# A six-layer decoder on one core: first statistics and normalising inside the weights' block, ones set by Pool, gates behind the split of x

## What is computed

```python
def _L0_attn_ref(hidden_states, Wq, Wk, Wv, Wo, gate):
    q, k, v = hidden_states @ Wq.T, hidden_states @ Wk.T, hidden_states @ Wv.T
    q = q * cos + rotate_half(q) * sin            # k likewise
    k_feat, q_feat = elu(k) + 1.0, elu(q) + 1.0
    memory = einsum('bhsd,bhse->bhde', k_feat, v)
    mem_out = einsum('bhsd,bhde->bhse', q_feat, memory) / denom
    attn = softmax(q k^T * scale) v
    g = sigmoid(gate)
    combined = g * mem_out + (1.0 - g) * attn
    return combined @ Wo.T

x = x + _L0_attn_ref(_layernorm(x), ...)          # layer 1: attention_linear
x = x + _L0_xattn_ref(ctx_512, _layernorm(x), ...)
x = x + _L0_ffn_ref(_layernorm(x), ...)
x = x + _L1_attn_ref(_layernorm(x), ...)          # layers 4 and 5: attention_layers
x = x + _L1_xattn_ref(_layernorm(x), ctx_512, ...)
x = x + _L1_ffn_ref(_layernorm(x), ...)
```

## Time and profile before

| | us |
|---|---|
| median of 3 runs | 3126.85 (3123.44 to 3128.61) |
| the profiled execution | 3120.07 |
| its span in the trace | 3118.0 |
| weights' block of attention_linear, by its rows | 3.4 to 25.6 |
| start of the main block to the first projection | 26.4 to 46.6 |
| weights' block of attention_layers | 1550.8 to 1615.3 |

### The profile page before, as it was taken

One profiled execution on the slowest core, in us unless ns is written; L12 is line 12 of the kernel. 1 busy time (PEld: TensorE's weight loads), 2 busy tenths in 40 slices (PEclk: granted clock), 3 DMA queues, 4 the chain that ended last, 5 costly groups with the idle time before them and its releaser, 6 DMA issues. The chain is left out here.

```text
span 3118.0 us, 34900 instructions
## 1 busy us (share of the span) xinstructions
PE 2474.1 (79%) x12662; PEld 1641.7 (53%) x12662; DVE 1844.8 (59%) x2916; ACT 1240.6 (40%) x1869; POOL 849.6 (27%) x1197
## 2 busy tenths in 40 slices
PE   5899989863532342999727999999999969999999
PEld 4454545321211122999624445545555537888887
DVE  4666665628977851777556777566555525444443
ACT  2343434328645531666411434334333313333332
POOL 1222222215567754333252343000111110000000
PEclk8899999975665565999858999999999978999999
DMA  2313132227222133899676656333433314001000
GB/s 92 85 42 82 42 82 45 68 86 283 73 68 80 52 96 121 283 305 302 213 206 158 153 155 160 92 95 91 119 97 88 99 52 178 14 28 41 1 28 14
DMA packets 200953, 340.40 MB, mean 109 GB/s; under 512 B 28810, under 2 KB 60426, under 8 KB 198755
## 3 DMA queue, kind: packets, MB, share of 16 engines
q1 hardware_dynamic: 177250, 299.80, 31.9%
q0 software_dynamic: 20480, 37.87, 4.7%
q10 hardware_dynamic: 3072, 0.79, 0.1%
HBM read 182.30 MB, written 109.05 MB: 93 GB/s over the span
## 5 line engine op out<-in xcount | busy, mean ns | idle before, releaser
L739 DVE TENSOR_REDUCE at_negmax<-at_ps 128x2 f32<-128x1024 f32 (+3 forms) x256 | 259.1, 1016 | 116.1 <-PE at_ps L505 59.4
L652 ACT ACTIVATE at_probs<-at_ps 128x1024 f32<-128x1024 f32 (+3 forms) x256 | 221.7, 866 | 265.4 <-PE at_ps L520 262.2
L1320 DVE TENSOR_REDUCE a_negmax<-a_ps 128x2 f32<-128x1024 f32 x128 | 155.2, 1217 | 134.0 <-PE a_ps L1060 133.3
L1816 ACT ACTIVATE gr_act_signs<-gr_signed,gr_test 128x512 bf16<-128x512 f32 x248 | 177.3, 716 | 133.2 <-POOL gr_test L2122 102.0
L59 PE MATMUL ff_ps<-ff_xnT_hi,ff_s_hi 128*128 128x512 f32 x512 | 200.8, 392 | 2.7 <-DVE ff_xnT_lo L2639 2.7
L60 PE MATMUL ff_ps<-ff_xnT_lo,ff_s_hi 128*128 128x512 f32 x512 | 200.2, 391 | 0.0
L61 PE MATMUL ff_ps<-ff_xnT_hi,ff_s_lo 128*128 128x512 f32 x512 | 200.1, 391 | 0.0
L520 PE MATMUL at_ps<-at_qk 98*128 98x512 f32 (+3 forms) x512 | 171.9, 418 | 16.9 <-DMA at_qk<-at_mrow 6.6
L2671 DVE TENSOR_TENSOR ff_hid<-ff_hid,ff_ps 128x512 f32<-128x512 f32 x64 | 44.0, 688 | 238.6 <-ACT ff_hid L2614 238.6
L1206 ACT ACTIVATE a_probs<-a_ps 128x1024 f32<-128x1024 f32 x128 | 130.8, 1023 | 136.5 <-PE a_ps L1076 136.0
L500 PE MATMUL at_ps<-at_qk 96*128 96x512 f32 (+3 forms) x512 | 163.1, 382 | 19.5 <-DVE at_xnT_lo L795 8.9
(11 more groups left out here) (399 smaller groups left out, 6566.9 us busy)
## 6 DMA issues: line engine op xcount, KB each, us to landing
at_qk<-at_part SPq DMA_DIRECT2D x384, 128.0 KB
ex_raw_gu<-in_L_ffn_w_gate_up_dram SPq DMA_DIRECT2D x32, 1024.0 KB
a_qk<-a_part SPq DMA_DIRECT2D x192, 128.0 KB
slot_rows<-gr_zeros SPq DMA_DIRECT2D x16, 1024.0 KB
ex_rows<-slot_rows SPq DMA_DIRECT2D x32, 512.0 KB
ex_raw_d<-in_L_ffn_w_down_dram SPq DMA_DIRECT2D x32, 512.0 KB
out_rows<-ex_y SPq DMA_DIRECT2D x32, 512.0 KB
gr_aside_raw<-in_L_ffn_W_dram SPq DMA_DIRECT2D x48, 256.0 KB
```

Source lines behind the costliest of these rows:

```text
L652: act.activation(probs[:, t % 2, 2 * w:2 * w + 2, lo:S], banks(("kq", g, s), lo), ACT.Exp, scale=SCALE).then_inc(free(("kq", g, s)), 1)
L739: dve.reduce_max(negmax[:, g % 2, :].rearrange("p (j t) -> p j t", t=NT)[:, 2 * w:2 * w + 2, t], banks(("qk", g, s), 0, width(g, t)), AX.X ...
L1320: dve.reduce_max(negmax[:, g % 2, :].rearrange("p (j t) -> p j t", t=NT)[:, 2 * w:2 * w + 2, t], banks(("qk", g, s)), AX.X, negate=True).t ...
L1816: act.activation(act_signs[:, j, :], src, ACT.Sign, scale=-1.0, bias=against, accum_out=total[:, i, j:j + 1]).then_inc(counted_to[j], 1)
```

## The change

- `load_weights`: ACT copies Wo's banks (it counts them on a new semaphore `plain_done`, for which nobody waits); DVE does nothing for them. This holds for both weights' blocks.
- `attention_linear`: the statistics of the first x run on DVE behind bank 7, its normalising behind banks 12 to 15, and Pool's part by `pool_aside`. The buffers and semaphores for it are allocated ahead of `load_weights`.
- Main block: `setup` is split into `ones_set` (DVE, for PE's first work) and `rows_set`; the rows of ones in `qk` are written by Pool, and PE waits for them only at its first scores that use them (g = 0). The gates move from the start of ACT's and DVE's lists to step -2. There ACT takes exp(-gate) behind the two copies of q and k, and DVE works out g and 1 - g ahead of its first product with cos; ACT's wait for them moves to step -1.

```diff
@@ load_weights, scalar and vector @@
-                if jobs[n][2] is None:
-                    continue
                 act.wait_ge(turned, u + 1)
-                act.copy(jobs[n][1][:, c, r * 512:(r + 1) * 512], ps[:, u % 8, :]).then_inc(high_done, 1)
+                act.copy(jobs[n][1][:, c, r * 512:(r + 1) * 512], ps[:, u % 8, :]).then_inc(plain_done if jobs[n][2] is None else high_done, 1)
...
-                if jobs[n][2] is None:
-                    dve.wait_ge(turned, u + 1)
-                    dve.tensor_copy(jobs[n][1][:, c, cols], ps[:, u % 8, :]).then_inc(low_done, 1)
-                else:
+                if jobs[n][2] is not None:
@@ attention_linear, ahead of load_weights @@
+        def first_norm(dve, u):
+            if u == 2 * NC - 1:
+                statistics(dve, 0)
+            if u >= 3 * NC and u - 3 * NC < NT:
+                layernorm(dve, 0, u - 3 * NC)
+
+        load_weights(nc, env, f"{tag}_w", [(wq, *wqT), (wk, *wkT), (wv, *wvT), (wo, woT, None)], also=lambda sp: load(sp, 0),
+                     pool_aside=lambda pool: rstds(pool, 0), dve_aside=first_norm)
@@ tensor @@
                 if s == 0:
                     pe.wait_ge(mx_in, 32 * (g + 1))
+                    if g == 0:
+                        pe.wait_ge(rows_set, 1)
...
-            pe.wait_ge(setup, 2)
+            pe.wait_ge(ones_set, 1)
@@ scalar @@
-            act.wait_ge(const_in, 16 * 3)
-            act.activation(gate_e[:], gate_e[:], ACT.Exp, scale=-1.0).then_inc(gates, 1)
-            act.wait_ge(gates, 2 + 2 * HC)
             for g in STEPS:
+                if g == STEPS[0] + 1:
+                    act.wait_ge(const_in, 16 * 3)
+                    act.activation(gate_e[:], gate_e[:], ACT.Exp, scale=-1.0).then_inc(gates, 1)
+                if g == -1:
+                    act.wait_ge(gates, 2 + 2 * HC)
@@ vector @@
-            dve.memset(ones[:], 1.0).then_inc(setup, 1)
-            dve.memset(qk[KROWS:KROWS + 2, :, 1].bitcast(F32), 1.0).then_inc(setup, 1)
...
-            statistics(0)
-            for t in range(NT):
-                layernorm(0, t)
+            dve.memset(ones[:], 1.0).then_inc(ones_set, 1)
             for g in STEPS:
                 b, c = g // NC, g % NC
+                if g == STEPS[0] + 1:
+                    gate_shares()
@@ gpsimd @@
-            rstds(0)
+            pool.memset(qk[KROWS:KROWS + 2, :, 1].bitcast(F32), 1.0).then_inc(rows_set, 1)
+            pool.wait_ge(rows_set, 1)
```

More of the change, by code:

```diff
@@ L112, in load_weights @@
         loaded = [sem(f"loaded{i}") for i in range(2)]
-        turned, high_done, low_done = sem("turned"), sem("high_done"), sem("low_done")
+        turned, high_done, low_done, plain_done = sem("turned"), sem("high_done"), sem("low_done"), sem("plain_done")
+        assert all(low is not None for _, _, low in jobs[:-1]) and jobs[-1][1].shape[1] <= 8
         block = ctx.enter_context(nc.Block())
@@ L877, in load, with statistics, layernorm, rstds @@
             sp.dma_start(xs(b), x_tiles[b]).then_inc(xs_in, 16)
-        load_weights(nc, env, f"{tag}_w", [(wq, *wqT), (wk, *wkT), (wv, *wvT), (wo, woT, None)], also=lambda sp: load(sp, 0))
+        stats, mv, rstd, carrier = sb("stats", [P, NT, 6]), sb("mv", [P, NT, 2]), sb("rstd", [P, NT]), sb("carrier", [P, 1])
+        stat, rstd_done, xn_done = sem("stat"), sem("rstd_done"), sem("xn_done")
+        def statistics(dve, b):
+            dve.wait_ge(xs_in, 16 * (b + 1))
+            for t in range(NT):
+                dve.bn_stats(stats[:, t, :], xs(b)[:, t, :]).then_inc(stat, 1)
+            dve.wait_ge(stat, 3 * NT * b + NT)
+            dve.memset(carrier[:], 0.0)
+            for t in range(NT):
+                dve.bn_aggr(mv[:, t, :], stats[:, t, :]).then_inc(stat, 1)
+            dve.wait_ge(stat, 3 * NT * b + 2 * NT)
+            for t in range(NT):
+                dve.tensor_scalar(mv[:, t, 1:2], mv[:, t, 1:2], EPS, None, ALU.add).then_inc(stat, 1)
+        def layernorm(dve, b, t):
+            dve.wait_ge(rstd_done, b + 1)
+            dve.tensor_scalar(xs(b)[:, t, :], xs(b)[:, t, :], mv[:, t, 0:1], rstd[:, t:t + 1],
+                              ALU.subtract, ALU.mult).then_inc(xn_done, 1)
+        def rstds(pool, b):
+            pool.wait_ge(stat, 3 * NT * (b + 1))
+            pool.tensor_tensor(rstd[:], mv[:, :, 1], env.minus_half[:, 0:NT], ALU.pow).then_inc(rstd_done, 1)
+        def first_norm(dve, u):
[5 more added lines that the diff above has]
+                     pool_aside=lambda pool: rstds(pool, 0), dve_aside=first_norm)
         xnT, oT = pair("xnT", [P, NC, S]), sb("oT", [P, NC, S])
@@ L981, in attention_linear @@
         res_in, res_out, const_in = sem("res_in"), sem("res_out"), sem("const_in")
-        setup, gates, stat, rstd_done, xn_done = sem("setup"), sem("gates"), sem("stat"), sem("rstd_done"), sem("xn_done")
+        ones_set, rows_set, gates = sem("ones_set"), sem("rows_set"), sem("gates")
         xT_ready, xT_hi, p_ready, v_ready = sem("xT_ready"), sem("xT_hi"), sem("p_ready"), sem("v_ready")
@@ L1297, in _ @@
         def _(dve):
-            def statistics(b):
-                dve.wait_ge(xs_in, 16 * (b + 1))
-                for t in range(NT):
-                    dve.bn_stats(stats[:, t, :], xs(b)[:, t, :]).then_inc(stat, 1)
-                dve.wait_ge(stat, 3 * NT * b + NT)
-                dve.memset(carrier[:], 0.0)
-                for t in range(NT):
-                    dve.bn_aggr(mv[:, t, :], stats[:, t, :]).then_inc(stat, 1)
-                dve.wait_ge(stat, 3 * NT * b + 2 * NT)
-                for t in range(NT):
-                    dve.tensor_scalar(mv[:, t, 1:2], mv[:, t, 1:2], EPS, None, ALU.add).then_inc(stat, 1)
-            def layernorm(b, t):
-                dve.wait_ge(rstd_done, b + 1)
-                dve.tensor_scalar(xs(b)[:, t, :], xs(b)[:, t, :], mv[:, t, 0:1], rstd[:, t:t + 1],
-                                  ALU.subtract, ALU.mult).then_inc(xn_done, 1)
             def maxima(g, s):
@@ L1370, in linear_reciprocals, with gate_shares @@
                 dve.reciprocal(spare(m)[:, 0, t * P:(t + 1) * P], spare(m)[:, 0, t * P:(t + 1) * P]).then_inc(l_rec, 1)
[L1372 to L1386 removed]
+            def gate_shares():
+                dve.wait_ge(gates, 1)
+                dve.tensor_scalar(gate_e[:], gate_e[:], 1.0, None, ALU.add).then_inc(gates, 1)
+                dve.wait_ge(gates, 2)
+                for j in range(HC):
+                    quarter = slice(j * HD, (j + 1) * HD)
+                    dve.reciprocal(g_sig[quarter, :], gate_e[quarter, :].rearrange("p (c j) -> p j c", j=HC)[:, j, :]).then_inc(gates, 1)
+                dve.wait_ge(gates, 2 + HC)
+                for j in range(HC):
+                    quarter = slice(j * HD, (j + 1) * HD)
+                    dve.tensor_scalar(g_not[quarter, :], g_sig[quarter, :], -1.0, 1.0, ALU.mult, ALU.add).then_inc(gates, 1)
+            dve.memset(ones[:], 1.0).then_inc(ones_set, 1)
             for g in STEPS:
                 b, c = g // NC, g % NC
+                if g == STEPS[0] + 1:
+                    gate_shares()
                 for s in range(PAIRS):
@@ L1408, in _ @@
                     if c == 1 and 1 <= b + 1 < B and s < NT:
-                        layernorm(b + 1, s)
+                        layernorm(dve, b + 1, s)
                     if out_unit(g, s):
@@ L1427, in _ @@
                 if c == 0 and 1 <= b + 1 < B:
-                    statistics(b + 1)
+                    statistics(dve, b + 1)
                 if out_unit(g, PAIRS):
@@ L1474, in _ @@
                 if c == 0 and 1 <= b + 1 < B:
-                    rstds(b + 1)
+                    rstds(pool, b + 1)
 def alloc_consts(nc, env, ctx):
```

15 lines of the change are left out of this document (removed).

## The result

The changed kernel takes 3106.64 us (median of 4 runs, 3101.4 to 3107.24), against 3127.73 us for four runs of the kernel before in the same session (3123.44 to 3133.76). The ratio is 0.9918, 95% interval 0.99 to 0.9935. Put against the median that the forecast started from, that is 3126.85 x 0.9918 = 3101.2 us: 25.6 us less, where 16.4 were forecast. The kernel is faster, as forecast, and by more than the range allowed (its lower end was 3105). The profiled execution took 3106.85 us, with a span of 3104.6 against 3118.0.

What follows compares the result with a forecast made beforehand. Stages run one behind another, so one path of waits through DVE, PE and ACT bounds the kernel. First stage -12.5, clock -1.5 and second weights' block -2.4 make -16.4 us: 3126.85 to 3110.5 us, range 3105 to 3117.

Steps and rivals of the forecast that it cites:

- End of the first block: First weights' block: DVE ends at 25.07 instead of 25.63, so the block ends 0.56 us earlier.
- Start of PE: Main block: PE starts transposing x at 26.1 instead of 39.92, -13.8 us.
- PE's possible 1.3 us of late start: Main block: a gap like DVE's could start PE at 27.4, making its term -12.5; left to the range.
- The split and the clock of the transposes: Transposes of x: no waits tile by tile, -0.65 us; upper clock level, -1.5 us.
- The clock of the projection: First projection: if the upper level holds, up to 2.8 us more gain; left to the range.
- rival on the clock: Transposes and projection at the upper level: -19.2, chance 0.20; or no gain from the clock: -14.9, chance 0.24.
- The gates: Ahead of the first product with cos: exp and nine small instructions now stand on the path, +1.95 us.
- Pool in DVE's way: Main block's start: Pool's writing of rows slows DVE's low parts of x, +4.4 us, 3114.9; chance 0.05.
- The second block: Fourth layer's weights' block: four copies of 0.59 us leave DVE's list, -2.4 us.
- my argument that all had landed in time: Second weights' block: DMAs moved nothing from 1604 to 1607, so the gathered rows would not delay DVE's earlier additions.
- Slower by ACT: Second weights' block: odd waits ahead of ACT's four copies; slower by 6.3 us from 9.2 us per copy; chance 0.02.

Runs made afterwards that it cites:

- e8: The changed kernel with the gates back at the head of ACT's and DVE's lists; ratio 0.994 to the kernel before.
- e7: The changed kernel with statistics and normalising of the first x back at the main block's start, Pool's rows of ones behind Pool's part; ratio 0.9965 to the kernel before.
- g1: The changed kernel with the copies of Wo back on DVE in the fourth layer's weights' block alone; ratio 0.9929 to the kernel before.
- g2: The changed kernel repeated unchanged in a later session; ratio 0.9931 to the kernel before.
- Wo alone: The kernel before with only ACT's copies of Wo's banks in both weights' blocks, run twice; ratios 0.9985 and 0.9984 to the kernel before.
- e1: The changed kernel repeated unchanged in a later session; ratio 0.9935 to the kernel before.
- e5: The kernel before, unchanged, compared with itself for a second trace on another chip; ratio 0.9992.
- f3: The kernel before with 110 extra transposes of the identity at the head of PE's list in the main block; ratio 0.9995 to the kernel before.
- f2: The changed kernel repeated unchanged on the same chip as a trace of the kernel before; ratio 0.9946 to the kernel before.

## Why the prediction was right or wrong

- **End of the first block, -0.56.** Right in kind, a little small. DVE had no wait for x; the statistics began at 16.31, a microsecond ahead of the 17.3 forecast, and Pool's 1.02 us at 19.64 cost nothing. `ones` is written at 25.37 in the mean of four traces, against 26.14 in three: -0.77.
- **Start of PE, -13.8.** Right: 39.65 to 25.51 in the means, -14.1. PE's possible 1.3 us of late start did not occur; it began 0.14 us behind `ones`.
- **The split and the clock of the transposes, -0.65 and -1.5.** Right: 16 transposes in 1.97 us at 1.00 of the clock, and from the first transpose to the projection 4.58 us instead of 6.68, -2.10 against the -2.15 of both terms. Projection at 30.10, forecast 30.6. *The Trainium skill's page "TensorE: Matmul & The Clock Gate", Part 4 (PE-mode transpose), would have these transposes at the lower level. The trace has them at the upper one, behind a block of nothing but transposes.*
- **The clock of the projection,** left to the range. It isn't a fixed term: 0 to 14 slow matmuls in the changed kernel, 8 to 14 before. In the mean 12 against 7; the 48 matmuls' own time, first start to last, was 13.19 us before and 12.44 after, 0.75 less. So neither rival on the clock is the right one; a trace of before in which the projection ran unusually slow isn't the mean from which to count.
- **The gates, +1.95.** Right: ACT's copy ended 1.94 us before the product in every trace in that order (43.78 to 45.72) and 0.11 us before it in the kernel before, so the term is +1.83. The prediction's premise that nothing on DVE's list needed what wasn't there at the end of the weights' block doesn't hold for the gates: their load is issued in the main block, and e8 waits for it. With this term the first stage closes: -14.1 - 2.1 + 1.8 - 0.75 = -15.15, and the means of the first product differ by 15.1.
- **Pool in DVE's way, a rival.** It did not occur: 2.36 us for two low parts, 1.2 each, beside a memset of 5.22 us. *It is as the page "GPSIMD Engine Reference" of the Trainium skill, Key points, has it: one of DVE's operands was in PSUM.* That Pool's memset can stop DVE is shown by e7, where it held up a normalising instruction for 5.0 us. So the rival was a real one, and the changed kernel avoids it, because DVE has normalised x before the memset starts.
- **The second block, -2.4.** Mis-sized: 1.7 between the traces of before and after, 2.0 between g1 and g2, and 0 in the session where the gathers end the block. The term took 0.59 us for each of four copies, the time until the next instruction; three of them stood between additions that wait for one another, and cost 0.4 each. As for the 0, my argument that all had landed in time rested on a trace in which ACT had held everything up by 12 us.
- **Slower by ACT.** Did not occur. ACT's odd idle times are there (4.93 and 8.53 us), but none stands ahead of the copies of Wo.

**The step that failed** is the last one, the range: "the 2.5 us by which medians of three such runs may miss". The places and most of the costs were right. Summed by the traces, the change gives 15.1 + 1.7 = 16.8 us, close to the 16.4 forecast; that is partly luck, since a second block mis-sized by 0.7 and a projection clock left out of the sum (0.75) cancel. The times give 19.6 ± 0.9, and the first comparison, against which the forecast stands, 3 us more still by its means and 6 by its ratio. So there are two misses. The range took 2.5 us for what medians of a few runs may be off; the four comparisons of one change scatter by 8 us, and the interval of the first alone is 0.0035 x 3127 = 10.9 us wide. And some 3 us of gain aren't in the two places where the change acts; Wo alone shows the same (5.0 ± 1.0 in the times, 3.0 in the two blocks, or 4.0 with the first product's mean of 58.62 in place of the block's end). One trace can't find 3 us there. From the first product to the second block the three traces of before took 1489.0 to 1498.0 us and the four of the changed kernel 1488.8 to 1498.8; from the second block to the end 1500.2 to 1502.7 and 1502.4 to 1506.1. The means differ by -1.0 and +3.0 us, so these stretches show no gain. What makes them scatter isn't shown; in the first of them the granted clock was 0.82 or 0.83. With one trace per kernel and session I can't say whether these 3 us are there or are chance; that is left open.

## What to carry to other kernels

Ask of each wait on the path what the waiting work needs, and place it where that is there: statistics that need only x can run beside the weights, and about 7 us came from this one move. When a long instruction leaves an engine's list, look which load it hid; here the next item (the gates) would have waited for a DMA, so both had to move. When you give a long write to Pool, look what DVE does at that time: the same memset of 5.2 us cost nothing beside subtractions that read from PSUM and 5.0 us beside the normalising. When you cost a removed instruction by its row, look whether the next one would have waited anyway. For a difference of 0.5%, make the range at least as wide as the interval of the measurement itself, and read the sum from several traces of the kernel before, because the clock alone moved one and the same milestone of the changed kernel by 2.5 us (44.72 to 47.27).

## What was unexpected

- The second weights' block of the same kernel took 55.1 us in one session and 62.8 to 62.9 us in three others. The difference is idle time of ACT ahead of its last two banks of Wv (0.27 and 0.27 us there, 4.5 to 5.3 and 8.5 to 9.2 us here), while the DMA engines are nearly all busy (a share of 0.98 from 20 to 40 us behind the block's start in the changed kernel's first trace). That alone doesn't make it: the share was 1.02 in e1, which has no such idle time. It is in the kernel before too (e5: 5.09 and 7.83).
- A Pool memset on two partitions held up one DVE instruction on 128 partitions for its whole length (e7: 5.52 us instead of 0.54), and left others untouched.
- PE's clock stayed at the upper level through 2.7 us without work in f3 and fell while it was working; in f2 it stayed up through a gap of 2.6 us and the projection.
